# One exponential per block in place of four beside the logarithms, and expert work over quads 39 to 231 in place of 41 to 230

## The chip, the cores and the metric

The kernel runs on one core of a Trainium2 chip. The metric is the device time of one execution in microseconds (us); of several executions of a kernel the median is given. Engines are named PE (TensorE), DVE (VectorE), ACT (ScalarE), POOL (GpSimd) and SP (SyncE, which issues DMAs here).

## The reference, cut to what matters

The input is `x` of shape (4, 1024, 256): 4 sequences of 1024 steps with 256 channels. It is normalised, goes through a recurrence with 16 states for each channel, and through a layer of 8 experts; the output is `x + s * silu(experts)`.

```python
dt = soft_clamp(softplus(x @ Wdt.T + bdt), 0.001, 0.1, 0.5)      # log and exp, then tanh
A = -exp(soft_clamp(A_log, -5.0, 5.0, 0.5))
dA = exp(soft_clamp(dt[..., None] * A, -8.0, 8.0, 0.5))          # the decays: tanh, then exp
def step(h, inp):                                                # 1024 times, one after the other
    h = dAt * h + dBt * xt[..., None]
    scale = minimum(20.0 / (sqrt(sum(h * h, axis=(1, 2))) + 1e-8), 1.0)
    h = h * scale
    return h, einsum('bdn,bn->bd', h, Ct) + Dp * xt
# experts: 2 of 8 for each token, capacity 1280
h = gelu(einsum('ecd,edf->ecf', exp_batches, c_fc))
exp_out = einsum('ecf,efd->ecd', h, c_proj)
out = cb_weight @ exp_out
```

The decay of every step, channel and state is `exp(16 * tanh(...))` in the kernel; it needs a tanh and an exponential of 1024 x 128 x 128 numbers. A gelu is needed for the experts, and an exponential and a logarithm for the softplus. All of these run on ACT, which holds one set of function tables at a time; an `ACT_TABLE_LOAD` brings in another.

## The kernel before, in words

**The recurrence is on DVE.** Its loop runs over the 1024 steps. The names of time are: a *quad* is 4 steps (256 of them), a *block* 16 steps or 4 quads (64 of them), a *half* 64 steps or 16 quads. Each step is a fixed chain of small instructions (L700 to L758), with one power on POOL (L528). At the last step of quad n DVE waits, ahead of L746, for `u_done`, that is for the inputs of quad n+1.

**ACT and PE prepare each quad and do the expert work between.** The order on each is written out in the program, in loops over `blk` and `q` (the quad within the block); both loops walk over the same table `by_quad`. PE does for each quad: 4 transposes of the decays (L1258) into one of two banks, 4 matmuls with `pick` that spread the inputs (L1264), into a single bank `ps[2]`, and then what `by_quad` has for this quad. Ahead of the transposes in q 1 stands the output of an earlier block (L1222, L1226). PE waits for `decay_ready` at the start of a block, and for `u_done` of the quad before ahead of every L1264, since `ps[2]` is single. ACT does for each quad: the copy of the transposed decays (L1012), four copies of the inputs (L1019; the last one raises `u_done`), the evictions of the expert work in this quad (L1034 gelu of an up, L1038 copy of a turn, L1045 copy of a finished pair of downs), and 2 or 3 instructions of tanh for the next half (L887). Now and then come: L835 to L843 (exponential and logarithm of the time rates, in the first quad of a half), L847 and L850 (soft clamp), L857 to L859, L865, L873, L879; and at the end of a block L963, which brings the inputs of the next block out of PSUM.

**The decays' exponentials** are `decay_op` (L902): one instruction of 128 x 2048 for one block. In steady state four of them are needed for each half. Two are issued in the last quad of the half before (L1077 and the loop behind it), the other two in the first quad of the half, between L835 and the logarithms. The explicit load at L1077 brings the set that has both exponential and logarithm, so that L843 needs none of its own.

```python
elif blk + 4 < NBLK:                                   # the last quad of a half
    act.wait_ge(tanh_done, blk // 4 + 2)
    a.preload_act_table_set("natural_log_exp_and_others")
    for c in range(2):
        decay_op(1 - f, c)
```

**The expert work** is a list: for each of 8 experts a turn of the rows, then 5 times 4 ups (weight 4), a turn (weight 1) and 2 downs (weight 8). It is laid evenly over quads MOE_AT to MOE_QUADS. In the text, u is an up, D a down, T a turn; "uu" is a quad with two ups. An expert's first weights `wf` come by an SP DMA at the start of the block in which its first up stands; the rows of the first turn come only when all 64 scattering DMAs of POOL (L511, one in every second step from 16 to 142) have landed. The results are fetched by POOL from step 930 on (L517).

Of the kernel before, what the change touches and what calls it, by code (L numbers as in the profile page):

```python
# [19 lines left out]
NB, NT, D, NS = 4, 1024, 256, 16  # L20
# [11 lines left out]
QUAD = 4  # L32
# [23 lines left out]
def build(nc, x, wdtT, bdt, wb, wc, a_log, dpar, w_g, c_fc, c_proj, out):  # L56
# [4 lines left out]
    with ctx:  # L61
# [237 lines left out]
        for m in range(NE):  # L299
            work += [("turn", m * TPE, 0, 1)]  # L300
            for i in range(m * TPE, (m + 1) * TPE):
                work += [("up", i, j, 4) for j in range(FC // 2)]
                work += [("turn", i + 1, 0, 1)] if (i + 1) % TPE else []
                work += [("down", i, c, 8) for c in range(2)]
        QUADS, MOE_AT, MOE_QUADS, COMBINE_AT, LAST_HALF = NT // QUAD, 41, 230, 237, 240
        n = 0
        total = sum(w[3] for w in work)
        by_quad = [[] for _ in range(QUADS)]
# [477 lines left out]
        def _(act):  # L786
            a = nc.scalar
# [41 lines left out]
            def rates_out(h, bank):  # L829


                act.wait_ge(z_ps, h + 1)
                flat = stage[:, h % 2, 0, :]
                for k in range(DH):
                    last = a.activation(flat[:, k * HALF * NB:(k + 1) * HALF * NB], ps[bank][:, k * HALF * NB:(k + 1) * HALF * NB],  # L835
                                        ACT.Relu, bias=bdt_sb[:, k:k + 1], scale=-1.0)
                last.then_inc(z_used, 1)
# [61 lines left out]
            def decay_op(f, c):  # L899

                part = tanhb[:, f, :, c * BLK:(c + 1) * BLK]
                a.activation(part, part, ACT.Exp, scale=16.0).then_inc(decay_ready, 1)  # L902
# [57 lines left out]
            def inputs_out_of_psum(n):  # L960

                act.wait_ge(x_ps, n + 1)
                a.activation(xin, ps[3][:, P:2 * P], ACT.Copy).then_inc(x_sb, 1)  # L963

            inputs_out_of_psum(0)
            def windows(n):

                act.wait_ge(cs_ready, n)
                act.wait_ge(y_done, n + 1)
                for b in range(NB):  # L970
                    last = a.activation(win[32 * b:32 * b + 32, :, QUAD - 1, DH * b:DH * (b + 1)], cs[32 * b:32 * b + 32, n % 2], ACT.Copy)  # L971
                last.then_inc(win_ready, 1)

            def y_out_of_psum(n):
                act.wait_ge(y_done, n + 2)
                act.wait_ge(y_out, n * 16 + 1)
                a.activation(ysb, ps[3][:, 0:P], ACT.Copy).then_inc(y_sb, 1)
# [18 lines left out]
            for blk in range(NBLK):  # L996
                half, f = blk % 2, blk // 4 % 2

                act.wait_ge(q_ready, blk * BLK + 1)
                if blk % 4 == 0:  # L1000
                    act.wait_ge(norm_ready, 2 * (blk // 4 + 1))
                a.activation(terms[:, half * BLK:(half + 1) * BLK, 2:4], be[:, span(blk * BLK, BLK), :],
                             ACT.Copy).then_inc(be_stage, 1)
                for q in range(QPB):
                    t = half * BLK + q * QUAD
                    quad = blk * QPB + q
                    if q == 0 and blk > 0:
                        windows(blk)
                    if q == 1:
                        y_out_of_psum(blk)  # L1010
                    act.wait_ge(ta_ps, quad + 2)
                    a.activation(da[:, t:t + QUAD, :].rearrange("p t d -> p (t d)"), ps[q % 2][:, :], ACT.Copy)\  # L1012
                        .then_inc(da_done, 1)

                    if q == 0:
                        act.wait_ge(be_stage, blk + 1)
                    act.wait_ge(tu_ps, quad + 1)
                    for j in range(QUAD):
                        last = a.activation(ur[:, t + j, :], ps[2][:, j * P:(j + 1) * P], ACT.Copy,  # L1019
                                            scale=terms[:, t + j, 3:4])  # L1020
                    last.then_inc(u_done, 1)
                    if blk % 4 == 0 and 0 < blk and q == 0 and blk // 4 + 2 < HALVES:
                        rates_out(blk // 4 + 2, 6)
                    if blk % 4 == 0 and 0 < blk and q == 0:
                        for c in range(2, 4):
                            decay_op(f, c)
                    if blk % 4 == 0 and 0 < blk and q == 0 and blk // 4 + 2 < HALVES:
                        logs_of(blk // 4 + 2)
                    for kind, i, j, _ in by_quad[quad]:
                        if kind == "up":  # L1030
                            if j == 0:
                                act.wait_ge(mm2_ps, i * 2 + 1)
                            act.wait_ge(mm1_ps, i * FC // 2 + j + 2)
                            a.activation(hid[:, 2 * j:2 * j + 2, :].rearrange("p c s -> p (c s)"), ps[4 + j % 2][:, :],  # L1034
                                         ACT.Gelu).then_inc(gelu_done, 1)
                        elif kind == "turn":
                            act.wait_ge(xt_tp, i + 1)
                            a.activation(xt.rearrange("p k s -> p (k s)"), ps[6][:, :], ACT.Copy).then_inc(xt_in, 1)  # L1038
                        elif j == 1:
                            act.wait_ge(mm2_ps, i * 2 + 3)  # L1040
                            if i == 0:
                                act.wait_ge(sent, 16 * 2 * TILES)
                            else:
                                act.wait_ge(ye_out, 16 * i)
                            a.activation(yrow.rearrange("p c d -> p (c d)"), ps[7][:, :], ACT.Copy).then_inc(ye_sb, 1)  # L1045
                    if quad == COMBINE_AT:
                        act.wait_ge(ye_out, 16 * NE * TPE)
                        act.wait_ge(mm2_ps, NE * TPE * 2 + 1)
                    if 0 <= quad - COMBINE_AT < 2 * CH:
                        weights_of(quad - COMBINE_AT)  # L1050
                    if 0 <= quad - COMBINE_AT - 1 < 2 * CH:
                        gate_of(quad - COMBINE_AT - 1)
                    if blk % 4 == 0 and blk > 0 and q == 1 and blk // 4 + 2 < HALVES:
                        b_and_c_out(blk // 4 + 2, 6)
                    if blk % 4 == 1 and q == 0 and 2 <= blk // 4 + 1 < HALVES:
                        sums_out(blk // 4 + 1, 6)
                    if q == QPB - 1 and blk + 1 < NBLK:
                        inputs_out_of_psum(blk + 1)

                    if quad < 3:  # L1060
                        last = tanh_part(11 * quad, min(11, 32 - 11 * quad), BLK, HALF)
                        if quad == 2:
                            last.then_inc(rest_done, 1)
                            act.wait_ge(rest_done, 1)
                    elif blk + 4 < NBLK and quad % 16 < 15:
                        if (blk % 4 == 0 and q == 0) or quad == 3:
                            act.wait_ge(th_ready, blk // 4 + 2)
                            act.wait_ge(ta_ps, blk // 4 * (HALF // QUAD) + 1)
                            if blk == 0:
                                act.wait_ge(xn_out, 16 * CH)  # L1070
                        first, end = [32 * (c - 3) // 12 if blk < 4 else 32 * c // 15 for c in (quad % 16, quad % 16 + 1)]
                        last = tanh_ops(1 - f, first, end - first)
                        if quad % 16 == 14:
                            last.then_inc(tanh_done, 1)
                    elif blk + 4 < NBLK:
                        act.wait_ge(tanh_done, blk // 4 + 2)
                        a.preload_act_table_set("natural_log_exp_and_others")  # L1077
                        for c in range(2):
                            decay_op(1 - f, c)
                    if q == 2 and blk < 3:  # L1080
                        decay_op(0, blk + 1)
                    if q == 2 and blk % 4 == 1 and 2 <= (blk + 3) // 4 < HALVES:
                        skip_of((blk + 3) // 4)
                    if blk % 4 == 2 and q == 1 and blk // 4 + 2 < HALVES:
                        soft_clamp(blk // 4 + 2)
                    if blk == 1 and q == 1:
                        rates_out(2, 6)
                        logs_of(2)
                    if blk == 1 and q == 2:
                        b_and_c_out(2, 6)  # L1090
                if blk % 4 == 0 and 2 <= blk // 4 + 1 < HALVES:
                    squares_of(blk // 4 + 1)
# [267 lines left out]
```

## Time and profile before

| what | us |
|---|---|
| median of 3 executions | 1633.51 (1630.07 to 1633.64) |
| the profiled execution | 1631.89 |
| its span, first to last instruction | 1630.2 |
| DVE busy | 1516.2 (93%) |
| PE busy (matmul) | 1282.2 (79%) |
| ACT busy | 1161.3 (71%) |
| POOL busy | 771.1 (47%) |
| mean granted clock of PE | 0.891 |

The span leaves out 1.7 us of the time. A busy share says how long an engine has an instruction in it; instructions of one engine overlap a little, so in the timeline the start of one instruction and the start of the next give the true pace. The granted clock is a share of 2.4 GHz; 0.50 is 1.2 GHz. Idle time of an engine is put down to what ended it.

### The profile page before, as it was taken

The page shows a single profiled execution, that of the slowest core. Times are in us where ns is not written, and L with a number is a line of the kernel's source. Part 1 is how long each engine was busy: PE and PEld are TensorE (multiplying, and loading weights), DVE is VectorE, ACT ScalarE, POOL GpSimd, SP SyncE. Part 2 cuts the span into 40 slices and gives each one's busy share as a digit, 9 for nine tenths or more (in the row PEclk, how much of TensorE's full clock was granted, in tenths as well). Part 3 has the DMA queues.
Part 4 walks back from the last instruction along what each step waited for, and adds up shares of the span by engine and source line. Part 5 has one row for each costly group of instructions (what it writes and reads, how often), then busy time and mean ns, then how long its engine had stood idle before and what let it go on. Part 6 is the DMA issues. An engine that isn't in the chain of part 4 may idle for free.

```text
span 1630.2 us, 34427 instructions
## 1 busy us (share of the span) xinstructions
PE 1282.2 (79%) x9628; PEld 1121.8 (69%) x9628; DVE 1516.2 (93%) x9684; ACT 1161.3 (71%) x2944; POOL 771.1 (47%) x1254
## 2 busy tenths in 40 slices
PE   5665445689899888989999997999989798945661
PEld 4554434578788777878878786888878688734550
DVE  6988888999999999999999999999999999987897
ACT  7887546577786868777776877778777777846550
POOL 4267766444444444444433344344444334468852
PEclk9767767789999999999989999999999999978795
DMA  9921111200120020120012002111201100014235
GB/s 344 322 70 47 46 41 43 96 18 24 42 68 31 18 74 24 37 74 24 24 42 69 17 30 67 37 31 35 64 16 32 63 27 18 18 42 152 81 93 163
DMA packets 85089, 104.56 MB, mean 64 GB/s; under 512 B 7712, under 2 KB 75936, under 8 KB 84896
## 3 DMA queue, kind: packets, MB, share of 16 engines
q1 hardware_dynamic: 76416, 84.82, 16.0%
q0 software_dynamic: 6144, 16.79, 3.2%
q8 instruction: 77, 1.26, 0.3%
q10 hardware_dynamic: 2336, 0.75, 0.2%
q14 instruction: 116, 0.95, 0.2%
HBM read 56.45 MB, written 45.88 MB: 63 GB/s over the span
## 4 chain that ended last, share of the span: by engine, by line
PE 46%; DVE 16%; POOL 15%; ACT 13%; issue 7%; DMA 1%; POOLq 0%; ACTq 0%; SPq 0%; DVEq 0%
PE ps L1292 15%; PE ps L1276 13%; PE ps L1264 8%; POOL arena L528 7%; PE ps L1258 4%; POOL xg L511 4%; ACT arena L902 3%; DVE arena L710 3%; DVE arena L736 3%; DVE arena L746 2%; DVE arena L758 2%; PE ps L1226 2%; DVE arena L705 2%; ACT arena L1019 2%; POOL wf L517 2%
## 5 line engine op out<-in xcount | busy, mean ns | idle before, releaser
L528 POOL TENSOR_TENSOR arena<-arena,neghalf 128x1 f32<-128x1 f32 x1025 | 595.5, 581 | 791.2 <-DVE arena L700 786.3
L710 DVE SCALAR_TENSOR_TENSOR arena<-arena 128x128 f32<-128x128 f32 x1024 | 362.3, 354 | 21.7 <-POOL arena L528 21.7
L1264 PE MATMUL ps<-arena,pick 128*128 128x128 f32 x2048 | 299.5, 293 | 63.2 <-ACT arena L1019 39.7
L1264 PEld LDWEIGHTS ps<-arena,pick 128*128 128x128 f32 x2048 | 275.9, 208 | 77.3 <-ACT arena L1019 64.6
L1276 PE MATMUL ps<-arena,wf 128*128 128x256 f32 x1280 | 309.4, 393 | 20.6 <-ACT arena L1034 8.8
L1019 ACT ACTIVATE arena<-ps,arena 128x128 f32<-128x128 f32 x1024 | 292.2, 374 | 29.9 <-PE ps L1264 28.0
L1292 PE MATMUL ps<-wp,arena 128*128 128x256 f32 x1280 | 304.7, 393 | 8.6 <-ACT arena L1034 5.5
L746 DVE CUSTOM_DVE_ANT_0 arena<-arena 128x128 f32<-128x128 f32 x1024 | 292.7, 286 | 11.7 <-ACT arena L1019 8.6
L736 DVE CUSTOM_DVE_ANT_0 arena<-arena 128x128 f32<-128x128 f32 x1024 | 298.4, 291 | 2.2
L705 DVE TENSOR_TENSOR arena<-arena 128x128 f32<-128x128 f32 x1024 | 288.7, 282 | 0.0
L1276 PEld LDWEIGHTS ps<-arena,wf 128*128 128x128 f32 x1280 | 245.0, 198 | 54.0 <-ACT arena L1034 9.5
L1292 PEld LDWEIGHTS ps<-wp,arena 128*128 128x128 f32 x1280 | 247.9, 199 | 43.0 <-ACT arena L1034 6.3
L758 DVE TRANSPOSE_TENSOR_REDUCE arena<-arena 128x2 f32<-128x64 f32 x1024 | 250.1, 244 | 23.0
L1258 PE MATMUL ps<-ident,arena 128*128 128x128 f32 x1024 | 206.5, 327 | 64.0 <-ACT arena L902 64.0
L715 DVE TENSOR_TENSOR_SCAN arena<-arena 128x2 f32<-128x2 f32 x1024 | 221.3, 216 | 27.9 <-POOL arena L528 27.7
L1258 PEld LDWEIGHTS ps<-ident,arena 128*128 128x128 f32 x1024 | 179.0, 244 | 92.7 <-ACT arena L902 70.8
L887 ACT ACTIVATE arena<-arena,a 128x256 f32<-128x256 f32 x480 | 217.0, 515 | 0.1
L1012 ACT ACTIVATE arena<-ps 128x512 f32<-128x512 f32 x256 | 153.5, 600 | 75.4 <-PE ps L1258 73.6
L700 DVE TENSOR_SCALAR arena<-arena 128x1 f32<-128x1 f32 x1024 | 150.0, 146 | 0.0
L1034 ACT ACTIVATE arena<-ps 128x512 f32<-128x512 f32 x160 | 96.0, 609 | 70.3 <-PE ps L1276 70.1
L902 ACT ACTIVATE arena<-arena 128x2048 f32<-128x2048 f32 x64 | 119.4, 1920 | 0.2
L1222 PE MATMUL ps<-ident,arena 128*128 128x128 f32 x128 | 30.7, 326 | 79.2 <-ACT arena L971 76.8
(149 smaller groups left out, 1334.0 us busy)
## 6 DMA issues: line engine op xcount, KB each, us to landing
xg<-zeros SPq DMA_DIRECT2D x10, 1024.0 KB, 10.3
xrow<-xg SPq DMA_DIRECT2D x40, 256.0 KB, 2.7
yg<-arena SPq DMA_DIRECT2D x40, 256.0 KB, 2.2
wf<-in_c_fc SPq DMA_DIRECT2D x8, 1024.0 KB, 5.2
wp<-in_c_proj SPq DMA_DIRECT2D x8, 1024.0 KB, 6.0
arena<-in_x SPq DMA_DIRECT2D x15, 512.0 KB, 7.4
xnd<-arena SPq DMA_DIRECT2D x8, 512.0 KB, 6.6
ys<-arena SPq DMA_DIRECT2D x64, 64.0 KB, 1.6
```

The costliest lines, as they stand in the source:

```text
L528: g.tensor_tensor(sv[:, slot, 1:2], mx, neghalf[:, 0:1], ALU.pow).then_inc(s_ready, 1)
L705: v.tensor_tensor(vv, hr[:, before, :], da[:, slot, :], ALU.mult).then_inc(v_ready, 1)
L710: v.scalar_tensor_tensor(hr[:, slot, :], vv, sv[:, before, 1:2], ur[:, slot, :], ALU.mult, ALU.add).then_inc(h_ready, 1)
L715: v.tensor_tensor_scan(horner, sv[:, before, 1:2].broadcast_to([P, 2]), terms[:, slot, 1:3], terms[:, slot, 0:1], ALU.mult, ALU.add).then_ ...
L736: v.tensor_tensor_reduce(out=junk[:, 0, :], in0=vv, in1=ur[:, slot, :], scale=2.0 / CLAMP ** 2, scalar=0.0, op0=ALU.mult, op1=ALU.add, acc ...
L746: v.tensor_tensor_reduce(out=junk[:, 1, :], in0=vv, in1=vv, scale=1.0 / CLAMP ** 2, scalar=0.0, op0=ALU.mult, op1=ALU.add, accum_out=ac[:, ...
L758: v.tensor_reduce(out=terms[:, slot, 0:2], in_=ac.unsqueeze(2).broadcast_to([P, 2, 32]), axis=AX.X, op=ALU.add, apply_transpose=True).then ...
L1019: last = a.activation(ur[:, t + j, :], ps[2][:, j * P:(j + 1) * P], ACT.Copy, scale=terms[:, t + j, 3:4])
L1258: last = t.transpose(ps[q % 2][:, j * P:(j + 1) * P], tanhb[:, f, :, s], ident[:, :])
L1264: last = t.matmul(ps[2][:, j * P:(j + 1) * P], pick[:, q * QUAD + j, :], xin, start=True, stop=True)
L1276: last = t.matmul(ps[4 + j % 2][:, c * TS:(c + 1) * TS], wf[:, k, (2 * j + c) * P:(2 * j + c + 1) * P], xt[:, k, :], start=k == 0, stop=k ...
L1292: last = t.matmul(ps[7][:, j * D:(j + 1) * D], hid[:, k, j * P:(j + 1) * P], wp[:, k, :], start=k == 0, stop=k == FC - 1)
```

## The change

The first two exponentials become one, without the explicit load. The two beside the logarithms go away. In place of these three, one stands at the end of the second quad (q 1) of the first, second and third block of each half, behind the tanh instructions. In the very first half the exponentials of blocks 2 and 3 move from q 2 to q 1 too. The expert work is spread over 192 quads in place of 189.

```diff
-        QUADS, MOE_AT, MOE_QUADS, COMBINE_AT, LAST_HALF = NT // QUAD, 41, 230, 237, 240
+        QUADS, MOE_AT, MOE_QUADS, COMBINE_AT, LAST_HALF = NT // QUAD, 39, 231, 237, 240
...
                     if blk % 4 == 0 and 0 < blk and q == 0 and blk // 4 + 2 < HALVES:
                         rates_out(blk // 4 + 2, 6)
-                    if blk % 4 == 0 and 0 < blk and q == 0:
-                        for c in range(2, 4):
-                            decay_op(f, c)
                     if blk % 4 == 0 and 0 < blk and q == 0 and blk // 4 + 2 < HALVES:
                         logs_of(blk // 4 + 2)
...
                     elif blk + 4 < NBLK:
                         act.wait_ge(tanh_done, blk // 4 + 2)
-                        a.preload_act_table_set("natural_log_exp_and_others")
-                        for c in range(2):
-                            decay_op(1 - f, c)
-                    if q == 2 and blk < 3:
-                        decay_op(0, blk + 1)
+                        decay_op(1 - f, 0)
+                    if (q == 2 and blk == 0) or (q == 1 and blk > 0 and blk % 4 < 3):
+                        decay_op(f, blk % 4 + 1)
```

How the order of instructions moves on ACT at two places. (After the change, lines behind L1023 have smaller numbers: L1031 is the gelu that was L1034, L1035 the turn's copy that was L1038, L1042 the downs' copy that was L1045.)

ACT at the change of a half, behind the last copies of quad 111, before the change. L1002 and L971 prepare the block, L1012 and L1019 are the copies of quad 112, and L835, L842 and L843 the time rates with their exponential and logarithm:

```order
L1077 ACT_TABLE_LOAD
L902 ACTIVATE arena<-arena 128x128x16 x2
L1002 ACTIVATE arena<-be 128x16x2
L971 ACTIVATE arena<-arena 32x16x2 x4
L1012 ACTIVATE arena<-ps 128x512
L1019 ACTIVATE arena<-ps,arena 128x128 x4
L835 ACTIVATE arena<-ps,arena 128x256 x2
L902 ACTIVATE arena<-arena 128x128x16 x2
L842 ACTIVATE arena<-arena 128x512
L843 ACTIVATE arena<-arena 128x512
L1034 ACT_TABLE_LOAD
```

The same place with the change:

```order
L902 ACT_TABLE_LOAD
L902 ACTIVATE arena<-arena 128x128x16
L1002 ACTIVATE arena<-be 128x16x2
L971 ACTIVATE arena<-arena 32x16x2 x4
L1012 ACTIVATE arena<-ps 128x512
L1019 ACTIVATE arena<-ps,arena 128x128 x4
L835 ACTIVATE arena<-ps,arena 128x256 x2
L842 ACTIVATE arena<-arena 128x512
L843 ACT_TABLE_LOAD
L843 ACTIVATE arena<-arena 128x512
L1031 ACT_TABLE_LOAD
```

Three of four exponentials are gone from here, and there are three table loads in place of two.

ACT in quads 117 and 118, the second and third quad of the second block of a half, before the change:

```order
L1012 ACTIVATE arena<-ps 128x512
L1019 ACTIVATE arena<-ps,arena 128x128 x4
L1034 ACTIVATE arena<-ps 128x512 x2
L887 ACTIVATE arena<-arena,a 128x4x64 x2
L1012 ACTIVATE arena<-ps 128x512
L1019 ACTIVATE arena<-ps,arena 128x128 x4
```

With the change:

```order
L1012 ACTIVATE arena<-ps 128x512
L1019 ACTIVATE arena<-ps,arena 128x128 x4
L1031 ACTIVATE arena<-ps 128x512 x2
L887 ACTIVATE arena<-arena,a 128x4x64 x2
L902 ACT_TABLE_LOAD
L902 ACTIVATE arena<-arena 128x128x16
L1012 ACTIVATE arena<-ps 128x512
L1019 ACTIVATE arena<-ps,arena 128x128 x4
L1035 ACTIVATE arena<-ps 128x512
```

A table load and an exponential now stand between the tanh of quad 117 and the two copies of quad 118 that PE and DVE wait for. The next gelu has a load of its own again. Over the whole program ACT has 43 table loads before and 124 with the change: 48 at L902, 44 at the gelu (13 before), 14 at L843 (1 before), 10 at L887 (9), 5 at L993 (2), and 3 early ones.

## Rows read from the trace of the kernel before

**Rows 1.** Page, part 1: busy us, share of the span, instructions.
```profile
PE 1282.2 (79%) x9628; PEld 1121.8 (69%) x9628; DVE 1516.2 (93%) x9684; ACT 1161.3 (71%) x2944; POOL 771.1 (47%) x1254
```

**Rows 2.** Waits of DVE, whole run: us, times, longest; timeline of its last one.
```profile
DVE arena L746 <- ACT arena L1019: 8.6, 11, 1.6
DVE arena L746 <- PE ps L1226: 3.0, 4, 1.3
...
1310.89 0.29 DVE L746 CUSTOM_DVE_ANT_0 arena<-arena 128x128 f32<-128x128 f32 x1 [1.57 <-ACT arena L1019]
```

**Rows 3.** Window: PE, PEld, DVE, ACT, POOL busy (count), PEclk, DMA share, GB/s.
```profile
1051.00:1142.00 91.00, 86.27 (x639) 76.79 (x640) 89.44 (x586) 71.57 (x180) 37.50 (x67) 0.96 0.12 38
```

**Rows 4.** Waits of PE from 360 to 1300 us.
```profile
PE ps L1258 <- ACT arena L902: 35.9, 10, 3.6
...
PE ps L1276 <- ACT arena L1034: 8.8, 3, 3.9
...
PE ps L1292 <- ACT arena L1034: 5.5, 3, 2.6
PE ps L1276 <- DMA wf<-in_c_fc: 3.8, 1, 3.8
PE ps L1264 <- ACT arena L1019: 3.4, 6, 0.7
```

**Rows 5.** Group of ACT by line: busy us, mean ns, idle before it.
```profile
L902 ACT ACTIVATE arena<-arena 128x2048 f32<-128x2048 f32 x64 | 119.4, 1920 | 0.2
```

**Rows 6.** ACT timeline at the change of a half: start, us, what.
```profile
812.70 1.28 ACT L1077 ACT_TABLE_LOAD   x1
814.00 3.71 ACT L902 ACTIVATE arena<-arena 128x2048 f32<-128x2048 f32 x2
...
821.04 3.74 ACT L902 ACTIVATE arena<-arena 128x2048 f32<-128x2048 f32 x2
```

**Rows 7.** PE timeline at the same place.
```profile
815.96 1.15 PE L1258 MATMUL ps<-ident,arena 128*128 128x128 f32 x4 [3.59 <-ACT arena L902]
816.91 1.91 PE L1264 MATMUL ps<-arena,pick 128*128 128x128 f32 x8
...
827.92 5.41 PE L1292 MATMUL ps<-wp,arena 128*128 128x256 f32 x16 [2.58 <-ACT arena L1034]
```

**Rows 8.** PE timeline of ordinary quads: one up, then the next quad.
```profile
779.21 1.06 PE L1264 MATMUL ps<-arena,pick 128*128 128x128 f32 x8
780.11 1.89 PE L1276 MATMUL ps<-arena,wf 128*128 128x256 f32 x8
781.84 0.71 PE L1258 MATMUL ps<-ident,arena 128*128 128x128 f32 x4
782.38 1.06 PE L1264 MATMUL ps<-arena,pick 128*128 128x128 f32 x8
```

**Rows 9.** ACT timeline of the same quads.
```profile
780.31 1.14 ACT L1019 ACTIVATE arena<-ps,arena 128x128 f32<-128x128 f32 x4 [0.30 <-PE ps L1264]
782.10 0.60 ACT L1034 ACTIVATE arena<-ps 128x512 f32<-128x512 f32 x1 [0.65 <-PE ps L1276]
782.59 0.89 ACT L887 ACTIVATE arena<-arena,a 128x256 f32<-128x256 f32 x2
783.39 0.71 ACT L847 ACTIVATE arena<-arena,dtbias 128x512 f32<-128x512 f32 x1
...
784.66 0.58 ACT L1012 ACTIVATE arena<-ps 128x512 f32<-128x512 f32 x1
```

**Rows 10.** PE behind another wait; window (columns of rows 3) at 816 us.
```profile
866.44 3.43 PE L1276 MATMUL ps<-arena,wf 128*128 128x256 f32 x8 [2.73 <-issue]
...
816.00:820.00 4.00, 4.00 (x16) 3.72 (x17) 4.00 (x29) 3.92 (x10) 1.67 (x3) 0.50 0.02 4
```

**Rows 11.** Timeline: POOL's last scatter, PE's first turn.
```profile
290.67 1.15 POOL L511 DMA_INDIRECT xg<-wf,slot_of  x1 [0.17 <-issue]
...
304.20 1.11 PE L1198 MATMUL ps<-ident,xrow 128*128 128x128 f32 x4 [4.02 <-DMA xrow<-xg]
```

## The prediction

> **What bounds the kernel now.** I read the shares first: DVE is busy 93% of the span, PE 79%, ACT 71% [rows 1]. That looks like a kernel bound by the recurrence on DVE, with room elsewhere. The windows correct this: in a stretch with expert work PE is busy 86.3 of 91 us and DVE 89.4, ACT 71.6 [rows 3]. The waits of DVE say who is late: 11 times ACT's input copies (8.6 us) and 4 times the output matmuls (3.0 us), the last time for 1.57 us at 1310.89 us [rows 2]. A chain that is still late there has no room in hand; every microsecond that PE and ACT lose before it is one that DVE waits. In the list of ACT's waits from 360 to 1300 us DVE doesn't occur, so the pair PE and ACT runs as fast as it can, slightly slower than DVE. PE's waits show what holds it: 35.9 us for the first exponential of a half, 14.3 us for a gelu (8.8 + 5.5), 3.8 for weights, and only 3.4 for the input copies [rows 4]. The last is the number that I expect to grow.
>
> **What goes away.** At a half's change ACT does a load, two exponentials, later two more [rows 6]. PE waits 3.59 us for the first [rows 7], and will again: a load and one exponential still stand there. The other three cost PE little by themselves, but they delay the gelus: that is the 14.3 us. With the change ACT gets there three exponentials (3 x 1.87 = 5.6) sooner and one load (1.3, by the starts 812.70 and 814.00) later, 4.3 us net, more than each of these waits (at most 3.9). I take all 14.3 as gone. Behind such a wait PE runs slowly: the eight matmuls of an up take 3.43 in place of 1.89 us [rows 8, 10], a quad's `pick` matmuls 1.91 in place of 1.06, and the clock from 816 to 820 us is 0.50, that is 1.2 GHz [rows 7, 10]. For the five or six gelu waits I add 8 us. Gain: **22 us**.
>
> **What comes.** ACT gets 81 loads more (124 for 43), by 1.28 us 104 us. Three times a half it now does, behind the tanh of a quad n, a load and an exponential: 1.30 + 1.92 = 3.2 us [rows 5, 6], which I call E. Does it hide? Time is counted from the start of the `pick` matmuls of quad n. On PE they take 0.90 (779.21 to 780.11), an up 1.73 (to 781.84), the transposes 0.54 (to 782.38) [rows 8]; a down is as many matmuls as two ups, 3.46; a turn about 0.6. With M for the expert work of a quad, a quad lasts 1.44 + M, and PE needs the inputs of n+1 copied at 2.88 + M(n) + M(n+1), since their bank is single.
>
> ACT starts a gelu 0.26 behind its up, at 2.9, a second (or a down's copy) at 4.6. Then 0.5 to the tanh, 0.8 for two of them (782.59 to 783.39), E 3.2, 0.5 for L1012, 1.14 for L1019 [rows 9]. So it is done at 9.0 behind one up, at 10.7 behind two ups or a finishing down, at 9.5 behind an up and a turn, at 7.7 behind a first down, which has no eviction. In the third block the soft clamp adds 1.27 (783.39 to 784.66) [rows 9]. PE's wait is the difference:
> - one up, then one up: 9.0 - 6.3 = 2.7
> - two ups, then two ups: 10.7 - 9.8 = 0.9; with the clamp 2.2
> - down, then one up: 10.7 - 8.1 = 2.7; with the clamp 4.0
> - two ups, then a turn alone: 10.7 - 6.9 = 3.8
> - up and turn, then a down: 9.5 - 8.7 = 0.8; with the clamp 2.1
> - first down, then second down: 7.7 - 9.8, none.
>
> The new table repeats every 24 quads, so the contents of the three places repeat every three halves. Quads 97, 101, 105: 0.9 + 2.7 + 4.0 = 7.6. Quads 113, 117, 121: 0.8 + 3.8 + 2.2 = 6.8. Quads 129, 133, 137: 2.7 + 0 + 2.1 = 4.8. Quads 48 to 223 hold the first kind four times, the second four, the third three: 30.4 + 27.2 + 14.4 = 72, and quad 225 is 2.7: **75 us**. Before quad 39 there is no gelu and no load between tanh and exponential; ACT is far ahead there, and I cost those at nothing.
>
> The slow clock behind these waits is bounded by 0 and by 1.54 (3.43 - 1.89) each. I take 1.5 for the eight of 3.8 us and more, which are as long as the waits of the rows, and 0.5 for the fifteen between 2 and 2.8: **20 us**.
>
> Here the Trainium skill speaks against the change. The trace has 1.30 us from the start of a load to the start of what follows it. The skill (ScalarE: Activation LUTs, section What ACT_TABLE_LOAD costs) gives about 1283 ns for the load and another 1380 ns for a drain, 2.66 us for each switch. By that E would be 4.6 us, and 30 places with a wait would cost some 40 us more; I go by the trace. Its section Table sets: the hidden batching unit asks to batch activations by set; the bursts before did so and the change gives it up.
>
> **The table of expert work.** The first turn waits for POOL's last scatter, at 290.67, and for the rows, till 304.20 [rows 11]. This doesn't depend on where the table begins, so PE now stands still at quad 39 in place of 41: it does two quads of 1.44 later (+2.9). By quad 226, 0.5% less of the work is done (554 us of ups and downs by rows 8: -2.8). Net **0**; early the chain is later and can stall DVE sooner. Before, the first up shared its quad with its turn for five of the eight experts, now for all; PE then waits for the turn's copy. And first ups no longer stand at the start of a block, where their weights were late once (3.8 us [rows 4]). Net **+3**. Behind 1310.89 DVE never waited, so some room was won before quad 226: **-5**, an estimate. The end (POOL's fetches from step 930) needs the last rows of quad 230; it is reached some 5 us after step 919, at 1.45 us a step in time, so nothing.
>
> **The sum**, against the profiled execution: 1631.9 + 75 + 20 - 22 + 0 + 3 - 5 = 1703. The median of the runs is 1.6 above it: **1704 us**, 4.3% slower. What this measurement tells from no change is about 0.3%, 5 us.
>
> **The rivals.**
> 1. *E hides and the bursts are gone: faster.* ACT is idle 19 of 91 us [rows 3], E adds at most 7 a half. If PE could run on during E, DVE's 11.6 us of waits [rows 2] would vanish: 1622. It decides at PE's wait ahead of L1264; it holds if the copies of quad n+1 come before PE has finished its expert work. Against it: one bank, and quads with only one up or a turn. Chance 0.10.
> 2. *Both balance.* Only the waits of 3.8 us and more are real, 32 us, and 22 to 30 are saved: 1634 to 1655. Chance 0.14, of which a third within 0.3%.
> 3. *ACT becomes the bound.* It was busy 71.6 of 91 us; with 5.4 loads more in a half, 78.5. If its idle share stays what it is, a half lasts 1.096 times as long, 9 us more, over eleven halves 99: 1733. For it: ACT and PE wait for each other in turn, so a share may hold better than my waits one by one. Chance 0.18.
> 4. *The compiler places fewer loads.* The order of instructions shows 124; no chance left.
>
> My forecast has 0.58. The range goes down to half of the 75, no slow clock and 30 saved (1641), and up to a slow clock of 1.5 behind all 23 waits and the small waits that follow (for L963, and for a bank's gelu, 3 us in three halves), with 14 saved: 1743. Leaving little out at either end I give 1642 to 1738. Faster 0.10, within 0.3% 0.05, slower 0.85.
>
> **What would show it.** Right: 124 loads; ACT busy near 1265 us; PE's waits at L1264 for L1019 near 75 us in place of 3.4; those for a gelu nearly gone; DVE's waits at L746 near 80 us, spread over the places behind quads 1, 5 and 9 of a half; a mean clock below 0.89; the wait of 3.6 for the first exponential unchanged. The sum is wrong if PE waits at L1264 for less than 30 us, or if DVE waits elsewhere, for instance on POOL.

## The result, and the profile after

The changed kernel takes **1708.33 us** (median of 4 runs, 1701.16 to 1712.92), the kernel before 1633.3 us beside it: a ratio of 1.0476, with a 95% interval of 1.0451 to 1.0502. It is 75 us slower; 71 were forecast. The profiled execution has a span of 1704.2 us and a mean granted clock of 0.887.

The page of the changed kernel, part 1:

```profile
PE 1306.5 (77%) x9628; PEld 1141.2 (67%) x9628; DVE 1516.8 (89%) x9684; ACT 1265.9 (74%) x3025; POOL 772.8 (45%) x1254
```

DVE does the same work in the same busy time as before [rows 1]; its share falls only because the span grew. ACT is busy 104.6 us more. Its groups of table loads and the exponential (busy us, mean ns of one, idle before):

```profile
L902 ACT ACTIVATE arena<-arena 128x2048 f32<-128x2048 f32 x64 | 122.4, 1913 | 0.6
L902 ACT ACT_TABLE_LOAD x48 | 61.6, 1283 | 0.4
L1031 ACT ACT_TABLE_LOAD x44 | 56.5, 1283 | 18.3 <-PE ps L1271 17.3
L843 ACT ACT_TABLE_LOAD x14 | 18.0, 1283 | 0.3
```

The 64 exponentials cost what they did; the loads are what is new. DVE's waits, whole run, line waited for, us in total, times, longest:

```profile
DVE arena L746 <- ACT arena L1019: 48.6, 43, 2.5
DVE arena L746 <- PE ps L1221: 36.1, 23, 3.3
DVE arena L715 <- POOL arena L528: 26.6, 63, 2.0
```

At L746 DVE now waits 84.7 us, where it waited 11.6 [rows 2]: these 73 us are the loss. The wait for POOL is no part of it (27.7 us before, 26.6 now). PE's waits say why the data come late, from the first turn to quad 226 (306 to 1478.1 us):

```profile
PE ps L1259 <- ACT arena L1019: 65.5, 35, 3.8
PE ps L1253 <- ACT arena L902: 43.5, 12, 4.0
PE ps L1271 <- issue: 17.2, 8, 2.7
PE ps L1259 <- ACT arena L963: 14.6, 23, 1.5
PE ps L1287 <- ACT arena L1031: 6.4, 8, 0.8
```

The same stretch of the kernel before, for which [rows 4] give a part:

```profile
PE ps L1258 <- ACT arena L902: 43.1, 12, 3.6
PE ps L1264 <- ACT arena L963: 12.2, 27, 1.2
...
PE ps L1276 <- issue: 8.0, 5, 2.7
...
PE ps L1264 <- ACT arena L1019: 3.6, 7, 0.7
```

The wait for the input copies ahead of the `pick` matmuls grew from 3.6 to 65.5 us. One of them, PE and ACT behind quad 117 (two ups, then a quad with a turn alone):

```profile
800.13 1.06 PE L1259 MATMUL ps<-arena,pick 128*128 128x128 f32 x8
801.02 0.60 PE L1193 MATMUL ps<-ident,xrow 128*128 128x128 f32 x4
801.46 0.75 PE L1253 MATMUL ps<-ident,arena 128*128 128x128 f32 x4
805.96 2.08 PE L1259 MATMUL ps<-arena,pick 128*128 128x128 f32 x8 [3.75 <-ACT arena L1019]
```

```profile
799.78 0.60 ACT L1031 ACTIVATE arena<-ps 128x512 f32<-128x512 f32 x1 [1.13 <-PE ps L1271]
800.29 0.89 ACT L887 ACTIVATE arena<-arena,a 128x256 f32<-128x256 f32 x2
801.18 1.28 ACT L902 ACT_TABLE_LOAD   x1
802.47 1.91 ACT L902 ACTIVATE arena<-arena 128x2048 f32<-128x2048 f32 x1
804.29 0.58 ACT L1012 ACTIVATE arena<-ps 128x512 f32<-128x512 f32 x1
804.77 1.14 ACT L1019 ACTIVATE arena<-ps,arena 128x128 f32<-128x128 f32 x4
```

PE has done its turn and its transposes by 802.2 and then waits 3.75 us, since ACT has the load and the exponential (801.18 to 804.29) ahead of the two copies. For this pattern 3.8 us were forecast. And the `pick` matmuls behind it take 2.08 us in place of 1.06.

So the loss goes through PE. From its first turn to the copies of quad 226 PE and ACT need 1174.6 us (303.5 to 1478.1) where they needed 1095.2 (304.2 to 1399.4): 79.4 us more. PE's waits make 58 of them. By the clock records of the trace PE stood at 1.2 GHz for 120 us of the stretch in place of 98; by half of the difference, an estimate, that makes 11 more. Some 10 are left over, and no run says what they are: PE does two quads more behind its turn (2.9 us), but by quad 226 it has done 0.5% less expert work (2.8 us), so these two cancel. DVE had 4.2 us in hand at quad 226 before (from the end of the quad's last copy to the L746 that needs it) and has 0.3 now.

### The profile page after: what moved, and what is told of

It is laid out like the page before. It is cut to its first block, busy times and chain, and to the rows that moved or that the text cites. A ratio compares the mean times of both kernels' runs of the same rounds, so it can differ in the third digit from the quotient of the medians.

```text
span 1704.2 us, 34508 instructions
## 1 busy us (share of the span) xinstructions
PE 1306.5 (77%) x9628; PEld 1141.2 (67%) x9628; DVE 1516.8 (89%) x9684; ACT 1265.9 (74%) x3025; POOL 772.8 (45%) x1254
## 4 chain that ended last, share of the span: by engine, by line
PE 45%; ACT 24%; POOL 15%; issue 8%; DVE 6%; DMA 2%; ACTq 0%; POOLq 0%; SPq 0%; DVEq 0%
PE ps L1287 15%; PE ps L1271 11%; PE ps L1259 9%; POOL arena L528 6%; ACT arena L902 5%; POOL xg L511 4%; PE ps L1253 4%; ACT arena L1019 3%; ACT L902 3%; PE ps L1221 3%; ACT arena L1031 2%; ACT arena L887 2%; ACT L1031 2%; POOL wf L517 1%; POOL wp L517 1%
## 5 line engine op out<-in xcount | busy, mean ns | idle before, releaser
L1259 PE MATMUL ps<-arena,pick 128*128 128x128 f32 x2048 | 313.7, 302 | 131.7 <-ACT arena L1019 109.4
L1259 PEld LDWEIGHTS ps<-arena,pick 128*128 128x128 f32 x2048 | 285.5, 215 | 151.3 <-ACT arena L1019 131.7
L710 DVE SCALAR_TENSOR_TENSOR arena<-arena 128x128 f32<-128x128 f32 x1024 | 357.9, 349 | 21.7 <-POOL arena L528 21.7
L746 DVE CUSTOM_DVE_ANT_0 arena<-arena 128x128 f32<-128x128 f32 x1024 | 292.7, 286 | 85.2 <-ACT arena L1019 48.6
L1271 PE MATMUL ps<-arena,wf 128*128 128x256 f32 x1280 | 309.1, 394 | 17.4 <-issue 17.2
L1019 ACT ACTIVATE arena<-ps,arena 128x128 f32<-128x128 f32 x1024 | 292.7, 374 | 38.9 <-PE ps L1259 37.2
L1287 PE MATMUL ps<-wp,arena 128*128 128x256 f32 x1280 | 308.8, 397 | 6.4 <-ACT arena L1031 6.4
L1271 PEld LDWEIGHTS ps<-arena,wf 128*128 128x128 f32 x1280 | 245.8, 199 | 51.0 <-issue 19.0
L1287 PEld LDWEIGHTS ps<-wp,arena 128*128 128x128 f32 x1280 | 251.2, 202 | 42.7 <-ACT arena L1031 8.3
L1253 PE MATMUL ps<-ident,arena 128*128 128x128 f32 x1024 | 209.1, 331 | 57.1 <-ACT arena L902 57.1
L715 DVE TENSOR_TENSOR_SCAN arena<-arena 128x2 f32<-128x2 f32 x1024 | 220.8, 216 | 26.8 <-POOL arena L528 26.6
L887 ACT ACTIVATE arena<-arena,a 128x256 f32<-128x256 f32 x480 | 217.1, 515 | 0.1
L1012 ACT ACTIVATE arena<-ps 128x512 f32<-128x512 f32 x256 | 153.8, 601 | 47.6 <-PE ps L1253 45.8
L1031 ACT ACTIVATE arena<-ps 128x512 f32<-128x512 f32 x160 | 93.1, 603 | 44.5 <-PE ps L1271 44.0
L902 ACT ACTIVATE arena<-arena 128x2048 f32<-128x2048 f32 x64 | 122.4, 1913 | 0.6
L736 DVE DVE_READ_ACCUMULATOR2_ANT arena<- 128x1 f32 x1024 | 83.4, 81 | 0.0
```

Source lines behind the costliest of these rows:

```text
L710: v.scalar_tensor_tensor(hr[:, slot, :], vv, sv[:, before, 1:2], ur[:, slot, :], ALU.mult, ALU.add).then_inc(h_ready, 1)
L736: v.tensor_tensor_reduce(out=junk[:, 0, :], in0=vv, in1=ur[:, slot, :], scale=2.0 / CLAMP ** 2, scalar=0.0, op0=ALU.mult, op1=ALU.add, acc ...
L746: v.tensor_tensor_reduce(out=junk[:, 1, :], in0=vv, in1=vv, scale=1.0 / CLAMP ** 2, scalar=0.0, op0=ALU.mult, op1=ALU.add, accum_out=ac[:, ...
L887: last = a.activation(dst[:, :, k, n_, :], src[:, :, k, :], ACT.Tanh, scale=a16[:, c:c + 1])
L1253: last = t.transpose(ps[q % 2][:, j * P:(j + 1) * P], tanhb[:, f, :, s], ident[:, :])
L1259: last = t.matmul(ps[2][:, j * P:(j + 1) * P], pick[:, q * QUAD + j, :], xin, start=True, stop=True)
```

## The experiments

All are read against the kernel before, run on the same chip beside them. The sizes in us that are put down to the clock are estimates, half of the difference in time at 1.2 GHz. Two theories stood at first. **W**: PE waits at one place, by what expert work stands in the quad and the next one. **B**: ACT's busy time sets the pace, so what counts is the number of loads.

### The two parts of the change alone

```diff
# x1: the change, but
-NT // QUAD, 39, 231,
+NT // QUAD, 41, 230,
# x2: the kernel before, but
-NT // QUAD, 41, 230,
+NT // QUAD, 39, 231,
```

> The exponentials one per block as in the change, the expert work back on quads 41 to 230. Theory W (PE waits ahead of the pick matmuls, by what expert work stands in the quad and the next): the contents at the second quads differ; the same differences (behind the first block's place 0.93 us of B and C matmuls counted for PE) sum to 53 us in place of 67, so PE's waits for the input copies fall from 65.6 to about 52 us, and the time from 1708 to about 1690 (range 1680 to 1700), the early stall of DVE at quad 42 gone. Theory B (ACT's busy time sets the pace, 81 loads): ACT has the same instructions, so the time stays at 1705 to 1711.

Measured: 1703.74 us (1.0433, 1.0415 to 1.045). PE's waits for the input copies are 54.2 us, and 52 were expected; the early room is back too (DVE has 8.4 us in hand at quad 42). But the time fell by only 4.6 us against the change, into neither range. PE now waits 23.6 us for L963 in place of 14.6:

```profile
PE ps L1259 <- ACT arena L1019: 54.2, 28, 3.9
PE ps L1253 <- ACT arena L902: 43.1, 12, 3.6
PE ps L1259 <- ACT arena L963: 23.6, 27, 2.6
```

A sum of waits at one line is right and still misses the time. My reading is that ACT's backlog, once there, is met at the next single buffer too. For the time, theory B came nearer.

> The exponentials as before, the expert work on quads 39 to 231. Theory W: no waits of the new kind; PE stands still at quad 39 instead of 41 for the first turn, so the room of 11 us that ACT has at quad 42 goes, 3 us more where a first up shares its quad with its turn; 1634 to 1642, about 1637. DVE's waits at L746 from 11.6 to about 15 us, beginning near quad 42 to 49. Rival T (the table carries most of the loss): 1670 or more.

Measured: 1624.6 us (0.995, 0.9933 to 0.9967), a miss: the table alone makes the kernel faster. Again, with twelve executions:

> The kernel before with the expert work on quads 39 to 231, again, for a narrower interval and on the same chip as the two others: 1620 to 1627, a ratio of 0.993 to 0.998 to the kernel before.

Measured: 1624.88 us (0.9974, 0.996 to 0.9988). So the table alone gives 0.3 to 0.5%, 6 to 8 us. DVE's waits at L746 fall to 7.3 us (3.5 in the second run's profile) although PE waits longer for turned rows:

```profile
PE ps L1258 <- ACT arena L902: 43.5, 12, 4.0
PE ps L1276 <- issue: 16.5, 7, 2.7
PE ps L1264 <- ACT arena L963: 7.4, 23, 1.3
PE ps L1276 <- ACT arena L1034: 6.8, 5, 2.2
PE ps L1264 <- ACT arena L1019: 6.6, 12, 0.6
```

The gelu waits are 6.8 us (8.2 in the second run's profile) where they were 14.3 [rows 4]; other expert work stands at the change of a half now, which I take for the reason. The weights, late once before, are on time, and PE stands at 1.2 GHz for 81 us in place of 98. The whole slowdown is thus the exponentials': 70.8 us (x1 against the kernel before), and the table, which gives 6 to 8 alone, gives nothing together with them: 1708.3 against 1703.7 us, if anything it costs a little (the intervals of the ratios lie end to end, 1.0451 and 1.045). The waits for the input copies go that way, 65.5 against 54.2 us: the table repeats every 24 quads and puts worse pairs of quads at the exponentials' places. The waits for L963 take back 9 of these 11 us.

### Loads without exponentials, exponentials without loads

```diff
# x3: the kernel before, and
+                    if q == 1 and blk > 0 and blk % 4 < 3:
+                        a.preload_act_table_set("exp_and_others")
# x6: the change, x7: the kernel before, both with
-                                         ACT.Gelu)
+                                         ACT.Tanh)
```

> The kernel before with 45 loads of the exponential's set added at the places where the change has its exponentials, and no exponential moved; each makes the next gelu load its own set again, so there are 125 loads, as many as with the change. Theory B: 105 us of ACT come on top: 1690 or more. Theory W: a load alone is 1.3 us there in place of 3.2; the differences sum to 18 us over 14 places, and the gelu waits of PE at the change of a half stay: 1650 (range 1640 to 1662).

Measured: 1676.72 us (1.0283, 1.026 to 1.0305): 44 us slower, between the two theories. The waits for the input copies are 18.2 us, as expected (18), but those for L963 are 26.9 in place of 12.2:

```profile
PE ps L1266 <- ACT arena L963: 26.9, 27, 2.6
PE ps L1266 <- ACT arena L1019: 18.2, 20, 2.1
```

> The changed kernel with a tanh in place of each gelu of the experts (so what the experts give is another function); tanh and exponential share a set, and 40 table loads are left of 124. The exponentials stand where the change puts them. Theory P (the place matters, 1.9 us each in front of the copies): by the differences PE's waits for the input copies sum to 36 us in place of 66, and the time is 1650 to 1665. Theory L (only the loads matter): the exponentials alone cost nothing there, 1615 to 1630. By the run with the loads alone (+44 us for 82 loads, 0.53 us each) the 84 loads fewer give 1708 - 45 = 1663.

Measured: 1621.64 us (0.9944, 0.9927 to 0.9962).

> The kernel before with the same tanh for gelu: 36 loads of 43 are left. Both theories: only a few loads behind the bursts go, 1625 to 1634; it is the base against which the run before this one is read. Theory P has the other 20 to 35 us above this one, theory L within 8 us of it.

Measured: 1624.03 us (0.9966, 0.9946 to 0.9987), 1 us below what was expected. **Without reloads the change costs nothing**: the intervals of the two overlap. The swap left the length of the instruction as it was (610 ns for one in x7, 609 in the kernel before). Theory P falls as to the time. Its waits are there all the same; x6, 306 to 1381 us:

```profile
PE ps L1259 <- ACT arena L1019: 33.1, 27, 2.4
PE ps L1253 <- ACT arena L902: 26.4, 12, 2.6
PE ps L1271 <- issue: 16.4, 7, 2.7
PE ps L1143 <- ACT arena L1035: 5.9, 4, 1.5
PE ps L1259 <- ACT arena L963: 5.5, 20, 0.3
```

33.1 us for the input copies, and 36 were expected. What I had left out is what else goes with the loads: the first exponential of a half no longer has a load in front (43.1 us of waits for it in x7, 26.4 here), the gelu waits are gone (11.2 us in x7), L963 waits for 5.5 us in place of 11.1, and PE is at 1.2 GHz for 47 us in place of 74. None of the 27 waits is longer than 2.4 us, where the change had 3.8. The stretch of PE and ACT is no longer either (1077.9 us, 1082.1 in x7), so the cost isn't merely hidden by DVE. One thing is not separated: x6 has the new table and x7 the old one. The table alone gave 6 to 8 us with the reloads; should it give them here too, the exponentials by themselves cost about as much. The kernel before with tanh and the new table was not run.

The three runs together exclude a fixed price for a load. Loads alone cost 44 us (82 of them: 45 at these places, the others at the gelus behind them), exponentials alone, with the new table, nothing, both 71 with the table of before. 84 loads more, between x6 and the change, cost 87 us, 1.03 us each; 82 in x3 cost 0.53 each.

The waits for the input copies show the same thing on a smaller scale. There were 7 of them before (3.6 us), 20 with the loads alone (18.2), 27 with the exponentials alone (33.1), 35 with both (65.5). Above the 3.6 us the two parts make 44 us, and both together 62. A time in hand that has to be used up first would give this: by the differences of the prediction ACT has, without E, between 5.3 us in hand (two downs) and 0.8 too little (a down, then one up, with the clamp). That is argued and not shown, since no run changes the time in hand alone; and a single exponential did not fit at most of the places, so this is not the whole reason why x6 lost no time. What carries the 44 us of the loads alone is settled only in part: the two waits above are 29 us of them, all waits of PE some 32, the clock has no part (96 us at 1.2 GHz for 98), and some 10 stay open, as with the change itself.

### Other places

```diff
# x4: the change, but
-                    if (q == 2 and blk == 0) or (q == 1 and blk > 0 and blk % 4 < 3):
+                    if (q == 2 and blk % 4 == 0) or (q == 0 and 0 < blk and blk % 4 in (1, 2)):
# x9: as x4, but for 0 < blk, blk % 4 == 0 at q == 1
```

> The change with its three exponentials moved by one quad: in the first block of a half to the third quad, in the second and third block to the first quad, behind which the output matmuls of the next quad give PE 1.5 us more to do. Instructions and loads of ACT are the same in number as with the change (124). Theory W: the differences sum to 12 us in place of 67, so PE's waits for the input copies fall to 10 to 20 us and the time to about 1650 (range 1635 to 1662). Theory B: 1705 to 1711.

Measured: 1677.18 us (1.0274, 1.0257 to 1.0291). Same instructions, same number of loads, 31 us less than the change: the place matters once the loads are there, which theory B denies. Theory W had expected 27 us more of a gain. The waits for the input copies are 21.7 us (10 to 20 expected), those for L963 24.2:

```profile
PE ps L1259 <- ACT arena L963: 24.2, 27, 3.3
PE ps L1259 <- ACT arena L1019: 21.7, 24, 2.6
```

> The change, with the exponential of a half's first block left in its second quad (PE's waits of the changed kernel there are 0.5 to 0.8 us), and the other two moved to the first quad of the second and third block. 124 loads. The run with other quads had put the first one into the third quad, two places ahead of the block's last copy (L963), and PE's waits for that copy rose from 14.6 to 24.2 us. If the backlog of ACT, reaching L963, did that, the waits for L963 fall back to 14 to 17 us, those for the input copies sum to about 15 to 22 us, and the time is 1660 to 1670. If not, it stays at 1675 to 1680.

Measured: 1667.32 us (1.0225, 1.0193 to 1.0258), in the expected range, but by half of the reason only:

```profile
PE ps L1259 <- ACT arena L1019: 32.8, 42, 2.5
...
PE ps L1259 <- ACT arena L963: 10.0, 23, 1.2
```

The waits for L963 fell by 14.2 us, to less than the 14 to 17 expected; those for the copies rose by 11.1, to more than the 15 to 22 expected, in more and shorter ones. Their sum fell by 3.1 us only. What moved is the clock: PE stands at 1.2 GHz for 100 us in place of 126. By half of the difference that would be 13 us; the stretch is 7.0 us shorter (1131.7 us for 1138.7), so the estimate by the clock is too large here. The step from x4 to x9 is itself small: 10 us by the medians, 0.5% by the ratios, whose intervals just overlap (1.0257 and 1.0258).

### The logarithm's set, and two versions that were to be better

```diff
# x10: the change, and
+                        a.preload_act_table_set("natural_log_exp_and_others")
                         decay_op(1 - f, 0)
# y1: one exponential there behind this load, decay_op(f, 1) between rates_out and logs_of,
#     decay_op(f, blk % 4 + 1) at q == 0 of blk % 4 in (1, 2); y2: the kernel before, but
-                        for c in range(2, 4):
+                        for c in range(1, 4):
...
-                        for c in range(2):
-                            decay_op(1 - f, c)
+                        decay_op(1 - f, 0)
# y1 and y2 both with the expert work on quads 39 to 231
```

> The change, with the explicit load of the set that has the logarithm too kept in the last quad of a half: the logarithm needs no load of its own, 114 loads in place of 124. At the change of a half ACT is 1.3 us less behind. If each load costs the mean (87 us for 84 loads by the two runs without reloads, 1 us), 10 loads fewer give 1698; if it is the chain of load, exponential and load in the middle of a half that costs, and the change of a half has slack, 1703 to 1708.

Measured: 1709.79 us (1.0473, 1.0434 to 1.0512). It lies above both expectations. Ten loads fewer give nothing, which agrees with slack at the change of a half and a loss in the middle of it. PE's gelu waits did fall, from 6.6 to 3.2 us, but it stood at 1.2 GHz for 128 us in place of 120.

> Expert work on quads 39 to 231; of a half's four exponentials one stands in the last quad of the half before (behind the load of the set with the logarithm), one between the time rates and the logarithms, and two behind the tanh of the first quad of the second and third block, with loads of their own: 96 loads. Theory P and L alike: the bursts are 3.8 us shorter, but two exponentials a half bring two loads each; with 1.6 us for each such place (the run with other quads: 52 us over 33 places against the table alone) 22 places cost 35 us and the shorter bursts give back 10: about 1650 (1635 to 1660). Rival: the bursts are what holds PE, then 1615 to 1624.

Measured: 1641.71 us (1.0081, 1.005 to 1.0112). Two places a half in place of three, both in first quads: 17 us more than the table alone. The time is in the expected range; PE waits for the input copies 27 times, 22.2 us.

> Expert work on quads 39 to 231, exponentials as before, but only the one that PE waits for stays in the last quad of a half; the other three stand between the time rates and the logarithms. No load more than with the table alone (45). The copies of the first quad of a half come 1.9 us sooner, the gelus behind the logarithms at the same time as before: DVE's waits at L746 (7.3 us with the table alone) fall to 3 to 6, the time 1620 to 1625. If PE gains too, because it starts on the next expert work sooner, 1616 to 1620.

Measured: 1638.62 us (1.0048, 1.0023 to 1.0073; single runs from 1631 to 1649), a miss: 14 us more than the table alone, from moving one exponential behind the copies of the half's first quad, with no load added. The profile that follows is of its slowest execution, 1648.93 us, so its sums are larger than those of the median. ACT's timeline of y2:

```profile
728.57 1.28 ACT L1077 ACT_TABLE_LOAD   x1
729.87 1.91 ACT L902 ACTIVATE arena<-arena 128x2048 f32<-128x2048 f32 x1
731.68 0.23 ACT L1002 ACTIVATE arena<-be 128x32 f32<-128x32 f32 x1
731.80 0.96 ACT L971 ACTIVATE arena<-arena 32x32 f32<-32x32 f32 x4
733.02 0.60 ACT L1012 ACTIVATE arena<-ps 128x512 f32<-128x512 f32 x1 [0.26 <-PE ps L1257]
734.79 1.14 ACT L1019 ACTIVATE arena<-ps,arena 128x128 f32<-128x128 f32 x4 [1.17 <-PE ps L1263]
...
736.51 5.54 ACT L902 ACTIVATE arena<-arena 128x2048 f32<-128x2048 f32 x3
...
744.54 1.08 ACT L1034 ACTIVATE arena<-ps 128x512 f32<-128x512 f32 x2
```

With the second exponential in front of L1002, ACT filled the time in which PE, at half clock (0.50 from 732 to 736 us in y2), did the first transposes and `pick` matmuls. Now ACT waits there, 0.26 + 1.17 us, and reaches the gelu 15.97 us behind the load; with the table alone it was 14.61 (below). At the ten changes of a half from 446 to 1295 us it waits 1.42 to 1.44 us there in y2, and never with the table alone.

```profile
719.46 1.28 ACT L1077 ACT_TABLE_LOAD   x1
...
734.07 1.09 ACT L1034 ACTIVATE arena<-ps 128x512 f32<-128x512 f32 x2
```

PE's gelu waits go from 6.8 to 13.4 us and the time at 1.2 GHz from 81 to 115 us. In this execution the stretch of PE and ACT is 21.6 us longer than with the table alone; PE's waits are 6.5 of them, and the clock by the estimate 17. The order of the kernel before was right here.

The last run takes the waits that the table brings (17.2 us, for turned rows) out of the faster version:

```diff
# z1: expert work on quads 39 to 231, exponentials as before, and
-            work += [("turn", m * TPE, 0, 1)]
+            work += [("turn", 0, 0, 1)] if m == 0 else []
...
-                work += [("turn", i + 1, 0, 1)] if (i + 1) % TPE else []
+                work += [("turn", i + 1, 0, 1)] if i + 1 < NE * TPE else []
```

> The kernel before with the expert work on quads 39 to 231 and, at the change from one expert to the next, the turn of the next expert's first rows ahead of the two last downs instead of in the quad of its first up, as within an expert. PE's eight waits of about 2.1 us behind the turn (17.2 us in the run with the table alone) go, apart from the very first. DVE waited only 3.5 to 7.3 us at L746 there, so no more than that can be won: 1618 to 1624, about 1621; if DVE alone set the pace, 1624 to 1625 as with the table alone.

Measured: 1622.53 us (0.996, 0.9945 to 0.9975). It is faster than the kernel before by 0.4%; against the table alone (0.9974, 0.996 to 0.9988, and 0.995, 0.9933 to 0.9967) the intervals overlap. DVE's wait for the input copies is down to 1.9 us, 2.7 us with all that it waits for at L746, and PE's waits for turned rows are gone but for the very first (0.7 us). The recurrence on DVE is the bound of this version, and I expect little more from the order of ACT's work; that was not tried further.

## Why the prediction was right, point by point

**The bound.** Right. PE and ACT together set the pace, and what PE lost came out at DVE: 79.4 us in the stretch, 73 us of waits at L746, 75 us in the median.

**E, 75 us.** Measured 65.5 - 3.6 = 62 us. The differences hold for each pattern outside the first block of a half: one up and one up 2.55 us (2.7 forecast), down and one up with the clamp 3.77 (4.0), two ups and a turn alone 3.75 (3.8), two and two ups with the clamp 2.17 (2.2), up and turn, then a down, with the clamp 2.09 (2.1), first and second down none (none). In the first block they were 0.46, 0 and 0.78 for 0.9, 0.8 and 2.7: PE has the B and C matmuls there too (0.93 us), and comes from a stretch at half clock. Over the four, four and three halves this is 11 of the 13 us too many.

**The slow clock, 20 us, and 8 for what goes.** Net 12 forecast; 11 by the estimate from the trace (120 for 98 us at 1.2 GHz, half of the difference). No run measures it by itself.

**The gelu waits, all 14.3 us gone.** 6.6 us are left (L1287 and L1271 for L1031), of another kind: the gelu that has its own load, behind an exponential. Of the forecast gain about half came, and the table alone halves these waits too (6.8 us in x2).

**The table, 0 + 3.** Mis-signed by itself: alone it gives 6 to 8 us. The step that failed is that I priced the first turn and the shared quads, and not what comes to stand at the change of a half. The waits for turned rows are 17.2 us for 8.0, as thought. That the early room goes was seen: 11.5 us in hand at quad 42 before, none after, and DVE waits from there on.

**The rest.** The room at the end, -5: 4.2 us before, 0.3 now, right. POOL's fetches and the end: right, nothing moved.

**The price of a switch, 1.30 us.** Right. In quad 117 the load starts at 801.18, when the last tanh ends (800.29 + 0.89), and the exponential at 802.47, 1.29 us behind it. The Trainium skill (ScalarE: Activation LUTs, section What ACT_TABLE_LOAD costs) adds a drain of about 1380 ns, 2.66 us for a switch; no row shows that drain, and with it the sum would have been some 40 us too long. The same page of the Trainium skill, in section Table sets: the hidden batching unit, asks to batch activations by set. The runs agree where a gelu follows: the loads alone cost 44 us (x3), the exponentials without loads nothing (x6). But ten loads fewer gave nothing at the change of a half (x10), and a longer batch there, with no load more, cost 14 us (y2).

**The rivals.** That E hides was wrong with the reloads and, for the time though not for the waits, right without them (x6). That both balance, with only the waits of 3.8 us and more real, was wrong: those of 2.55, 2.17 and 2.09 us stand in the trace each time. The loads were 124, as the order of instructions said. That ACT's busy time is the bound (1733) was wrong: x4 saves 31 us with the same instructions. Still the time follows the number of loads more than my waits said. That the sum came out within 4 us is in part luck, since errors cancel: 13 us too many for the places, 7 too many for the gelu gain (14.3 for 7.7), and some 10 in what the sum left out, the small waits of a backlog of ACT among them, which only the range took in.

## What to carry to other kernels

When two engines hand work to each other through single buffers, ask of each inserted piece whether it fits into the time that the receiver still has work for, quad by quad, and take a load and the instruction behind it as one piece. That gives the single waits well (3.75 us for 3.8), and the time only roughly: what goes away elsewhere counts as much (x6). A shift of a static table can win or lose by what falls together with the other period, so try it with each version of the order, and price the clock along with each wait. And two engines that wait for each other, and never for the third, are the place to look for the bound, whatever the busy shares say.

## What the runs showed that I had not expected

The costs don't add: loads alone 44 us, exponentials alone none (with the new table), together 71. A long instruction in front of a burst can be free because PE runs at 1.2 GHz just then (y2, 14 us for moving it). And two versions with almost the same total of waits (45.9 and 42.8 us for the copies and L963 in x4 and x9) differ by 10 us in the median: in the one PE stood at 1.2 GHz for 126 us, in the other for 100. The longest waits for L963 and for the copies are 3.3 and 2.6 us in x4, 1.2 and 2.5 in x9, and there are 27 and 24 of them in x4, 23 and 42 in x9: few long waits went with more time at the lower clock than many short ones. That is one pair of runs, which shows the two together and not that one causes the other.
